# Starting the shared expert's products between the norm stages of a cross-attention and mixture-of-experts kernel

## The reference

```
x = x + tanh(g_xattn) * (0.6 * sigmoid(si + sj + b) + 0.4 * layernorm(x))   # si, sj: projections of ctx_512
h = layernorm(x)
probs = softmax(h @ gate_w.T); top 4 of 16 experts, weights normalised to 1
y = sum over the 4 of w * (silu(h @ Wg_e) * (h @ Wu_e)) @ Wd_e              # 512 -> 2 x 384 -> 512
  + (silu(h @ Wg_s) * (h @ Wu_s)) @ Wd_s                                    # the shared expert, all tokens
x = x + tanh(g_ffn) * y
```

## Time and profile before

| what | us |
|---|---|
| median of three runs | 723.48 |
| the profiled execution's own time | 728.89 |
| its span, first to last instruction | 727.2 |
| TensorE busy | 635.8 (87%) |
| VectorE busy | 524.4 (72%) |
| GpSimd busy | 321.5 (44%) |
| ScalarE busy | 313.7 (43%) |
| mean granted TensorE clock | 0.981 of full |

### The profile page before, as it was taken

How to read it: one execution, slowest core, us unless ns; L and a number is a source line. 1 busy time by engine, 2 the same in 40 slices (tenths; PEclk the granted TensorE clock), 3 DMA queues, 4 the chain that set the end, 5 groups by cost and what they waited for, 6 DMA issues and landing times.

```text
span 727.2 us, 18242 instructions
## 1 busy us (share of the span) xinstructions
PE 635.8 (87%) x4586; PEld 391.3 (54%) x4587; DVE 524.4 (72%) x1303; ACT 313.7 (43%) x542; POOL 321.5 (44%) x505
## 2 busy tenths in 40 slices
PE   4402659999999799999999999999999999999991
PEld 3302445667656456656555556665665555565560
DVE  5699968877678586858878867678777888867110
ACT  2324483222234345444545454544544544554541
POOL 1345540000021447556465565656556456465532
PEclk9999989999999899999999999999999999999997
DMA  7651144201113777675867867777695785755432
GB/s 231 214 154 59 45 146 117 80 1 59 47 57 109 170 189 150 156 176 116 184 126 170 197 117 180 144 152 157 130 216 101 175 196 109 189 89 88 77 45 39
DMA packets 48524, 93.73 MB, mean 129 GB/s; under 512 B 7677, under 2 KB 15339, under 8 KB 48498
## 3 DMA queue, kind: packets, MB, share of 16 engines
q0 software_dynamic: 16128, 38.35, 28.6%
q1 hardware_dynamic: 32370, 55.07, 26.8%
HBM read 65.16 MB, written 28.24 MB: 128 GB/s over the span
## 4 chain that ended last, share of the span: by engine, by line
PE 73%; DVE 12%; issue 4%; ACT 3%; DMA 3%; SPq 2%; POOL 2%; DVEq 1%; POOLq 0%; ACTq 0%
PE gu_ps L1124 41%; PE bank L1151 19%; PE bank L1163 4%; PE bank L1138 4%; PE bank L1177 2%; DVE stats L678 2%; DVE wgu L883 1%; DMA dn_sc<-dn_scale_halves 1%; DVE act L950 1%; PE gu_ps L1088 1%; POOL mix_room L411 1%; ACT acth L570 1%; ACT xT L539 1%; DVE wdn L889 1%; PE bank L1091 1%
## 5 line engine op out<-in xcount | busy, mean ns | idle before, releaser
L1124 PE MATMUL gu_ps<-wgu,mix_room 128*128 x1728 | 305.5, 327 | 1.9 <-DVE tick L906 1.7
L1124 PEld LDWEIGHTS gu_ps<-wgu,mix_room 128*128 128x128 f16 x1728 | 166.4, 98 | 113.7 <-issue 7.4
L1151 PE MATMUL bank<-wdn,aT 128*128 (+1 forms) x792 | 185.9, 380 | 1.0 <-ACT aT L577 1.0
L577 ACT ACTIVATE aT<-bank 128x768 f16<-128x768 f16 x88 | 71.4, 811 | 156.5 <-PE bank L1138 156.5
L489 POOL DMA_INDIRECT out<-mix_room,idx_s x72 | 120.3, 1670 | 20.6 <-issue 20.3
L1151 PEld LDWEIGHTS bank<-wdn,aT 128*128 128x128 f16 x792 | 77.7, 98 | 85.7 <-issue 2.3
L468 POOL COPY idx_g<-room_b 128x1 int32 x72 | 58.5, 812 | 118.9 <-issue 99.1
L950 DVE SCALAR_TENSOR_TENSOR act<-gu_ps,wslot,sg x72 | 44.5, 618 | 87.8 <-ACT sg L563 75.9
L486 POOL COPY idx_s<-room_b 128x1 int32 x72 | 21.5, 299 | 181.8 <-DMA out<-mix_room,idx_s 111.6
L570 ACT ACTIVATE acth<-act 128x384 f16<-128x384 f32 x88 | 46.0, 523 | 121.3 <-DVE act L950 120.2
L471 POOL DMA_INDIRECT room_b<-token_rows,idx_g x72 | 76.5, 1063 | 10.8 <-issue 1.0
(11 more groups left out here) (161 smaller groups left out, 672.2 us busy)
## 6 DMA issues: line engine op xcount, KB each, us to landing
dn_sc<-dn_scale_halves SPq DMA_DIRECT2D x34, 384.0 KB
dn_raw<-in_L_ffn_down_packed SPq DMA_DIRECT2D x48, 256.0 KB
gu_sc<-gu_scale_halves SPq DMA_DIRECT2D x34, 192.0 KB
X<-in_x SPq DMA_DIRECT2D x4, 1024.0 KB, 11.0
token_rows<-room_a SPq DMA_DIRECT2D x16, 256.0 KB, 2.0
out<-X SPq DMA_DIRECT2D x4, 1024.0 KB, 4.5
gu_raw<-in_L_ffn_gate_up_packed SPq DMA_DIRECT2D x16, 192.0 KB
gu_raw<-in_L_ffn_gate_up_packed SPq DMA_DIRECT2D x16, 191.9 KB
```

The source lines that it names most:

```text
L577: nc.scalar.activation(aT[:, b].rearrange("p a c t -> p (a c t)"), at_ps, ACT.Copy).then_inc(aT_done, 1)
L1124: mm = nc.tensor.matmul(ps[b][:, 0:I], x(xp * HC + c), wgu[:, w, wp, c, col:col + I], start=(c == 0 and xp == 0 and wp == 0), stop=(c == H ...
L1151: mm = nc.tensor.matmul(y_ps[b][:, :], aT[:, b, ap, t, :], wdn[:, w, wp, t, :], start=(n == 0), stop=(n == 3 * IC - 1))
```

## The change

ctx and x are loaded from ScalarE's queue. The scales of all experts are one tile of 128 rows and 612 columns, split in five instructions instead of ten, and shared scales are stored and loaded ahead of the others. All 16 sigmoid tiles have a place of their own (in `xT`'s memory), and the scaled x is written in place, so neither waits for `attend`. ScalarE makes the high half from X itself with the norm's factors; the low half is made by GpSimd. TensorE transposes only tiles 0 to 3 before shared slots 0 and 1; tiles 4 to 15 are transposed and routed in slots 3 to 8, two in each, through one PSUM bank, and the shared down products use one y bank. The routing steps move to slots 9 to 13. The lists are made for all experts together, one pass for each of a token's four choices: a one-hot of its row, a one-hot of its slot (80 of them) times its number, 16 matmuls of 80 columns for each choice. The shift of the words in each gate/up part is folded into the two operations on them. Column lookups of the slots fall away. The diff, cut to its core:

```diff
@@ buffers
-        sig, xmix, xn = (mix_room[:, k] for k in range(3))
+        spare, xmix, xn = (mix_room[:, k] for k in range(3))
+        sig = xT[:, :].rearrange("p i a c t -> p i (a c t)").bitcast(F32)
...
+        SC_SH, SD_SH = G_GU * GU // P, IC * H // P
+        sc_cut = [0, SC_SH, SC_SH * NE, SC_SH * NE + SD_SH, (SC_SH + SD_SH) * NE]
...
@@ SP
-            for b in range(B):
-                sp.dma_start(ctxs[:, b * TB:(b + 1) * TB, :], ctx_t[b]).then_inc(ld_ctx[b], 16)
-            for b in range(B):
-                sp.dma_start(X[:, b * TB:(b + 1) * TB, :], x_t[b]).then_inc(ld_x[b], 16)
+            load_words(sp, sh_gu_packed, sh_dn_packed, 0)
             sp.wait_ge(vs, SPLIT_STEPS)
...
+            sp.wait_ge(st_sc_sh, 64)
+            load_scales(sp, 0, 0)
+            load_words(sp, gu_packed[0], dn_packed[0], 1)
             sp.wait_ge(st_sc, 64)
-            load_expert(sp, sh_gu_packed, sh_dn_packed, 0, 0)
-            load_expert(sp, gu_packed[0], dn_packed[0], 1, 1)
+            load_scales(sp, 1, 1)
@@ GpSimd
-                    nc.gpsimd.tensor_scalar(xmix[:, i % 2, :], X[:, i, :], lnA[:, i:i + 1], lnB[:, i:i + 1],
+                    nc.gpsimd.tensor_scalar(X[:, i, :], X[:, i, :], lnA[:, i:i + 1], lnB[:, i:i + 1],
...
+            def low_x(i):
+                pool.wait_ge(xn_ready, i + 1)
+                pool.wait_ge(xh_ready, i + 1)
+                nc.gpsimd.tensor_tensor(xhl[:, i % ROWS_AHEAD, 1, :], xn[:, i % 2, :], xhl[:, i % ROWS_AHEAD, 0, :],
+                                        ALU.subtract).then_inc(xl_ready, 1)
+            def normalised(b):
+                for i in range(b * TB, (b + 1) * TB):
+                    normalise(i)
+                    if i % TB:
+                        low_x(i - 1)
+                low_x((b + 1) * TB - 1)
...
             inverse_std(0, 2)
             scaled_x(1)
+            inverse_std(1, 0)
+            norm_factors(0)
+            normalised(0)
+            scaled_x(2)
+            inverse_std(1, 1)
+            norm_factors(1)
             inverse_std(0, 3)
+            normalised(1)
+            scaled_x(3)
+            inverse_std(1, 2)
+            norm_factors(2)
+            normalised(2)
+            inverse_std(1, 3)
+            norm_factors(3)
+            normalised(3)
@@ ScalarE
+            load_ctx(0)
+            load_ctx(1)
+            load_x(0)
+            load_ctx(2)
+            load_ctx(3)
+            for b in range(1, B):
+                load_x(b)
...
+                nc.scalar.activation(xhl[:, i % ROWS_AHEAD, 0, :], X[:, i, :], ACT.Identity, scale=xs2[:, i:i + 1],
+                                     bias=xm2[:, i:i + 1]).then_inc(xh_ready, 1)
...
             for b in range(B):
                 scores(b)
+            for i in range(TB):
+                high_x(i)
+            for i in range(TB):
+                copy_xT(i)
...
             for i in range(2, NT):
                 copy_aT(i - 1, (i - 1) % 2)
+                if i in WITH_X:
+                    copy_xT(2 * i - 2)
+                if i == 11:
+                    a.wait_ge(lsub_ready, 1)
+                    nc.scalar.activation(r_exp[:, :, :], lg[:, :, :], ACT.Exp).then_inc(exp_ready, 1)
                 activate(i, i % 2)
+                if i in WITH_X:
+                    copy_xT(2 * i - 1)
+                if i == 2:
+                    for k in range(TB, 2 * TB):
+                        high_x(k)
+                if i in WITH_X and 2 * i + 2 < NT:
+                    high_x(2 * i + 2)
+                    high_x(2 * i + 3)
@@ VectorE
+            def positions():
...
+                step(nc.vector.tensor_tensor(g_pos, rank.rearrange("p e i -> p i e"), r_gt[:, :, :], ALU.mult))
+                for i in range(NT):
+                    step(nc.vector.max(top8[:, i, :], g_pos[:, i, :]), wait=i == NT - 1)
...
+            def mark(j):
...
+                step(nc.vector.tensor_tensor(onehot[:, j % 2], pos_row[:, j, :].unsqueeze(1).broadcast_to([P, P, NT]), place,
+                                             ALU.is_equal), wait=False)
+                step(nc.vector.tensor_tensor(values[:, j % 2], pos_slot[:, j, :].unsqueeze(1).broadcast_to(by_slot),
+                                             place[:, 0:SLOTS, :], ALU.is_equal))
+                nc.vector.tensor_tensor(values[:, j % 2], values[:, j % 2], token1[:, :].unsqueeze(1).broadcast_to(by_slot),
+                                        ALU.mult).then_inc(onehot_ready, 1)
...
             x_factors(0)
+            x_factors(1)
             first_stats(2)
+            take_words(0, 0)
+            dequant(0, 0, 0, None)
             attend(0)
             x_factors(2)
+            for k in range(1, PARTS):
+                dequant(0, 0, k, None)
...
+                if i == 2:
+                    x_factors(3)
+                    attend(2)
+                if i == 4:
+                    attend(3)
+                if 5 <= i < 9:
+                    first_weights(i - 5)
+                if i == 9:
+                    route()
+                if i == 10:
+                    ranks()
+                    tables()
+                    positions()
+                if i == 11:
+                    token_weights()
+                    mark(0)
+                    mark(1)
+                if i == 12:
+                    mark(2)
+                    mark(3)
+                    slot_tables(0)
+                if i == 13:
+                    slot_tables(1)
                     lists()
+                if i == NT - 1:
+                    first_weights(PARTS)
+            for d in range(PARTS):
+                if d % 2 == 0:
+                    dequant(0, 0, None, d)
+                else:
+                    dequant(0, 0, None, d)
+                    activations(d // 2, d // 2, shared_w[:, 0:1])
+                    low_halves(d // 2, d // 2)
...
+            take_words(1, 1)
+            attend(1)
+            first_stats(3)
@@ TensorE
+                if isinstance(s, int) and 1 <= s <= NT:
+                    pe.wait_ge(acc_done, s)
...
+            for i in range(TB):
                 transpose_x(i)
                 if i:
                     route(i - 1)
+            pe.wait_ge(sig_ready, NT)
+            pe.wait_ge(dqg_ready, 1)
+            for i in range(2):
+                for half in range(2):
+                    shared_gate_up(i, half)
+            route(TB - 1)
             transpose_act(0, 0)
...
             for i in range(2, NT):
                 shared_gate_up(i, 0)
                 transpose_act(i - 1, 1 - b)
+                if i in WITH_X:
+                    transpose_x(2 * i - 2)
                 shared_gate_up(i, 1)
                 down(i - 1, 1 - b, 0)
+                if i in WITH_X:
+                    transpose_x(2 * i - 1)
+                    route(2 * i - 2)
+                if i == 10:
+                    count()
+                if i in (12, 13):
+                    list_tokens(2 * (i - 12))
+                    list_tokens(2 * (i - 12) + 1)
```

More of the change, by code:

```diff
@@ L998, in after_shared_slot @@
-                if i == 8:
-                    first_weights(0)
-                if i == 10:
-                    first_weights(1)
-                if i == NT - 4:
-                    lists()
-                if i >= NT - 3:
-                    first_weights(i - (NT - 3) + 2)
-            for i in range(2):
-                activations(i, i, shared_w[:, 0:1])
-            for i in range(2):
-                low_halves(i, i)
-            route()
-            add_y(0)
+                    positions()
@@ L1014, in _ @@
+            v.wait_ge(dqs, 1 + PARTS * (G_STEPS + D_STEPS))
+            nc.vector.memset(tick[:, 0:1], 0.0).then_inc(dq_ready, 1)
+            take_words(1, 1)
+            attend(1)
+            first_stats(3)
             for i in range(2, NT):
@@ L1016, in _ @@
                 low_halves(i, i % 2)
+                if i == 2:
+                    add_y(0)
                 add_y(i - 1)
@@ L1142, in down @@
                 pe.wait_ge(aT_done, s + 1)
-                if isinstance(s, int) and 2 <= s < NT + 2:
-                    pe.wait_ge(acc_done, s - 1)
-                elif not isinstance(s, int) or s >= 2:
+                shared = isinstance(s, int) and s < NT
+                if isinstance(s, int) and 1 <= s <= NT:
+                    pe.wait_ge(acc_done, s)
+                elif not isinstance(s, int) or s >= NT + 2:
                     pe.wait_ge(yev_done, s - 1 - NT)
@@ L1203, in _ @@
                 if i == 2:
+                    pe.wait_ge(dq_ready, 1)
                     down(0, 0, 0)
                 transpose_act(i - 1, 1 - b)
-                if i == 2:
-                    count()
+                if i in WITH_X:
+                    transpose_x(2 * i - 2)
+                if i in WITH_X and i > 3:
+                    route(2 * i - 3)
+                if i == 9:
+                    route(NT - 1)
                 if i == NT - 1:
```

349 lines of the change are left out of this document (140 added, 209 removed).

## The result

| | before | after |
|---|---|---|
| median, us | 724.55 | 757.06 |
| fastest to slowest run shown | 722.33 to 728.62 | 750.82 to 759.50 |
| ratio, 95% interval | | 1.041 (1.036 to 1.047) |
| the profiled execution's own time, span | 728.89, 727.2 | 759.50, 757.8 |

The forecast was 696 (685 to 709). Executions of the kernel before come in two groups (but for a single one of 1715 us), most at 722.3 to 726.3 us and fewer at 728.6 to 731.6, and the profiled one is of the second, so a gain read between traces is some 5 us larger than one read between medians.

The account below looks back on a forecast made before the run. Preamble bound by VectorE, GpSimd and ScalarE in turn, then TensorE. T 25.2 us earlier plus 2.5 in the routed part make 27.7: 701.2 for the profiled execution, 696 in the median, 8 in 10 within 685 to 709.

Parts of the forecast that it names:

- T: The moment routed slot 0 starts, 218.46 us before the change; forecast at 193.3, 25.2 us earlier.
- Step 7: Routed part: nearly all behind TensorE, expert 2's load wait stays; 2.5 us less waiting for late halves (0 to 4).
- A: Rival: GpSimd becomes the bound through low halves and normalising in slots 3 to 8; slower, 733 us; chance 0.04.
- D: Rival: stored rows, cw or expert loads arrive late, so T moves little; no gain, 723 us; chance 0.02.
- B: Rival: GpSimd's normalise and low-half ops wait for VectorE, or the clock falls at step 6's waits; 708 us; chance 0.2.
- step 6: Routing chain, now in slots 9 to 13, is late next: T 54.0 us after slot 10 starts, plus 1.5 for low clock.
- C: Rival: more is won, as the routing chain hides and the stalls of step 6 go; 685 us; chance 0.2.
- Step 1: Start: ctx and x loads first on ScalarE's queue, projections end at 25.4 instead of 26.88, 1.5 us earlier (0 to 4).
- Step 2: Preamble, mix in place and order: attend(0) 5.8 us instead of 7.2, VectorE through it at 39.0; three parts until 49.3.
- Step 3: Low halves on GpSimd: 1.2 us quiet, 1.6 beside VectorE's dequantising; shared slot 0 starts at 53.9 instead of 82.7.
- Step 4: Shared slots 0 to 2: slot 3 starts at 85.4 instead of 118.45, 33.0 us won.
- Step 5: TensorE's work in slots 3 to 15: net 4 us less; slots 3 to 8 at 7.5 each, lists 4 (2 to 8).

Follow-up runs that it names:

- e1: The kernel after with VectorE's program 80 instructions longer at its start, so its expert loop lies 80 further on: 719.15 us, ratio 0.993.
- e14: The kernel of e12, the loop 40 instructions further on, with more runs (six): 718.86 us, ratio 0.991.
- e12: The kernel after with VectorE's program 40 instructions longer at its start: 721.58 us.
- e13: e9 with list values laid out as in the kernel after, 40 wait instructions instead of 80, and wj_all ahead of the scale split: 709.77 us, ratio 0.980.
- e7: e5 with constants issued ahead of scale loads, the scale split earlier, and two orders about shared slots 0 to 2 changed: 717.26 us, ratio 0.989.
- e4: e1 with list values laid out as tile, slot, so the 80 columns a matmul reads are neighbours: 751.72 us.
- e9: e7 with x's loads back on SP's queue behind constants and scales, and the shared expert's words issued behind the split scales' stores: 716.24 us, ratio 0.986.
- e5: e1 with list values laid out as tile, slot, and VectorE's two ops writing in that same order: 721.11 us.
- e2: The kernel before with VectorE's expert loop moved 190 instructions on by waits in a never-taken branch: 764.99 us, ratio 1.056.
- e3: The kernel after with VectorE's expert loop moved 261 instructions on by waits in a never-taken branch: 768.32 us, ratio 1.059.
- e11: The kernel after with VectorE's program 20 instructions longer at its start: 757.96 us.

## Why the prediction was wrong, step by step

The profiled execution's own time was to be 701.2 and is 759.5: 58.3 us. T is late by 18.6 of them and the routed part is longer by 39.7.

- **Step 7, the routed part, is the one that failed most.** I wrote of the load it starts with "the change doesn't touch it", gave the back edge of VectorE's loop no term at all, and took 2.5 off. The loop's operations are the old ones less the shifts, and the time came back when the loop was moved (508.9 in e1, 507.1 in e14, 508.7 before). Its place in the program was touched by everything taken out ahead of it (63 instructions), and that cost 37. Of the 2.5 some may be there: e12 to e14 have 506.6 to 507.3, and their waits for high halves are 1.0 to 2.6 us, not 4.1. No rival had the mechanism. A (733 us) and D (723) stood on the slow side, but TensorE never waited for a low half in slots 3 to 8, and T waited 1.30 us for VectorE's last tick and for no rows or loads, so neither happened; B's second half did, the low clock at the waits of step 6 (0.75 from 170.5 to 202 us). The sign named for C, no wait before the first gather, came without C. To find it blind one would have had to count VectorE's instructions and ask what the place of its loop costs, which nothing in the trace of the kernel before tells; its page had only the queue's 14 packets to ask about.
- **Step 1, the start, was 25.4 (between 22.9 and 26.9) and came out at 29.9, later than before (26.9).** I gave the new queue a gain because it starts first. What the row did not tell me: gate_w, for which VectorE and ScalarE wait, was issued 3.4 us later, behind the scales, and landed 6.9 us after its issue, before 2.5; and ScalarE was held for 7.2 us by its own three issues of x. With x on SP's queue, behind the small loads, and the words later, e13 has 5.2 us to landing, ScalarE free at 3 us, and the projections end at 24.6.
- **Step 2** inherits 4.5 of that and adds 3.3: attend(0) was to end at 39.0 and ended at 46.8. VectorE waited 1.84 us for the shared expert's scales, a wait that I had left out, and the first part took 3.9 us, not 2.6. Attend itself took 5.8 us, as predicted. These 7.8 us are nearly all of the 8.0 that slot 0 is late.
- **Step 3** had the right price for a low half (1.15 to 1.60 us measured, 1.2 and 1.6 taken), though no row gave those two: they were a choice between the bounds 0.77 and 3.7. The port that the recorded step speaks of no run shows, only what VectorE's operations took beside GpSimd's. It was wrong for the other side: of VectorE's three parts beside it two took 5.8 and 5.9 us, not 3.2. I had GpSimd as the bound. It was through 12.1 us after attend(0), 1.5 sooner than forecast, and VectorE after 14.9, 4.6 later than forecast, so slot 0 waited for VectorE. That it is 15.1 us from attend(0) to slot 0, against 14.9 in the forecast, is luck.
- **Step 4**: 32.6 us from slot 0 to slot 3, forecast 31.5 (82.2 and 3.0 are 85.2, not 85.4). Right for the orders as they stood; e7 then showed that 7 us of it were two orders of my own.
- **Step 5**: slots 3 to 8 took 49.6 us, where the stated starts make 46.0 (six times 7.5 is 45.0; a slip of 1.0), through three waits for ScalarE (1.89, 0.82, 1.70). The lists took 10.1 us, beyond the upper bound of 8: the bound was scaled from columns alone, and the layout counts (80 and 158 ns in e4 and e1).
- **Step 6**: from slot 10 to T 61.3 us, forecast 55.5. The selection was waited for 1.72 (forecast 1.6), act(11) 3.42 (3.3), the last tick 1.30 (1.2). The first lists and the gather were not waited for (forecast 2.5 and 3.6, 6.1 together), because TensorE was late itself: by the lists, 6.1 more, and by the low clock about them, 0.75 of full in the mean. The nine rows of other work from 170.5 to 202 that ran slow took 7.2 us longer than the same work elsewhere (three groups of twelve matmuls 4.05, 3.47 and 4.02, not 2.11), where I took 1.5. These three differences make 5.7 of the 5.8.

What the change promised is partly real: with the loads and three orders mended (e13) T is 17.5 us earlier than in the trace before (201.0 against 218.46), of the 25.2 forecast, and the median is 14.6 lower, of 27.7.

## What to carry to other kernels

Ahead of any edit that adds or removes instructions before a hardware loop, count the instructions of each engine's loop and where it lies: loops of 322 and 334 instructions were fast or slow here by their place alone (38 and 41 us of the median), and a change's own effect can only be read with the place held. In a profile, "issue" pieces of several us at a back edge (3.2 to 7.1 here) together with more packets on the instruction queue (39 or 41 for 14) were its mark. Second, bulk loads on one engine's queue were not free here for the small loads on another's (gate_w took 6.9 to 8.4 us to land with x on ScalarE's queue, 4.8 and 5.2 with only ctx there, 2.5 in the kernel before, where SP's queue issued all of it), so read the landing times, not the issue times. Third, what is put in to move or pad something must itself be looked up in the trace (the waits of e9 held VectorE until 12.0 us).

## What the runs showed that I had not expected

- VectorE: an operation over 1280 2-byte elements took 0.82 us (e1), with its result at a step of 160 bytes 5.53 (e4), and with results side by side but one operand repeated along the innermost dimension 1.49 (e5).
- TensorE: an 80-column matmul with columns 32 bytes apart took 158 ns (e1), side by side 74 (e5) to 81 (e4).
- Waits that are already met are not free on VectorE: in e9 80 wait instructions lasted until 12.0 us. The semaphore they name was reached at 3.75 us, with GpSimd's last constant, so they took some 0.10 us each (an estimate: 8.3 us over 80; e9's chain has all 80, 0.09 or 0.10 us apart from 3.79 on but for one gap of 0.52).
- A branch back cost 3.2 to 7.1 us in the four badly placed loops (after, e2, e3, e11), and in the well placed ones the chain has no issue piece over 0.84 us behind T.
